# A graph network kernel: the early sorted tile of a step goes behind the first filter layer, in steps that have no same-source sums

## The chip, the cores and the metric

The kernel runs on one core of a Trainium2 chip. The time is the device time of one execution, in microseconds, as the median of three runs; lower is better. Engines are named as in the profile: PE is TensorE, DVE VectorE, ACT ScalarE, POOL GpSimd, SP SyncE.

## The reference

A continuous-filter convolution over a graph of 6250 nodes and 200000 edges, inside a residual block:

```python
h = jnp.maximum(_layernorm(x, axis=-1), 0.0)
x = atomic_embedding @ W_in                                  # atomic_embedding = h
W_ij = shifted_softplus(f_ij @ W_f1 + b_f1) @ W_f2 + b_f2    # 20 -> 128 -> 128 for each edge
W_ij = W_ij * f_ij_cutoff
x_ij = x[idx_j] * W_ij                                       # idx_j = dst, which is sorted
out = jax.ops.segment_sum(x_ij, idx_i, num_segments=N_ATOMS) # idx_i = src, which is not
return shifted_softplus(out @ W_o1 + b_o1) @ W_o2 + b_o2     # and + x at the end
```

## The kernel before

Edges are cut into 391 chunks of 512 (four groups of 128). For each chunk the kernel computes a filter in two layers, fetches the rows of `dst` out of a window of 42 nodes, multiplies both into a message, and adds the message to the rows of `src`. There are two ways for the last part:

- **Pool chunks** (283). TensorE multiplies each group's messages by a matrix that marks equal sources (`same_product`, L1327, the "same-source sums"), ScalarE takes the sums out (`take_sums`: L748 the fourth group, L749 the other three), VectorE makes the target rows (L1011, L1015), and GpSimd scatters them with four indirect DMAs that add into four accumulators in HBM (L613). The scatters of a chunk wait for its sums and its targets; each also waits until the one before it on its accumulator has landed. ScalarE's `take_sums` waits until the scatters of four chunks earlier have landed.
- **PE chunks** (108, those with `c % 25` in `ON_PE`, seven of 25). The messages are sorted into 14 bins on TensorE: seven *tiles* for each chunk, four matmuls of 386 columns each (`bin_up`, L1341), all into the one PSUM bank `binned_ps`. ScalarE empties it after each tile (`take_binned`, L758), and the next tile waits for that (`s_binned`). From the sorted tiles, node sums are made by `add_nodes` (L1360) and added by VectorE (L1059).

The program of each engine is written out step by step. Step `k` on TensorE works on several chunks at once; its order before the change:

1. same-source sums of chunk `k - 2`, if that is a pool chunk; the fourth group waits for the hidden layer of `k`
2. the *early* tile of this step (`late` is 0 in `sorts_at[k]`)
3. `filter_bias` of `k` (L1315, 32 rows, one matmul of 512 columns), which waits for the message of `k - 1` (`s_msg`), since both use bank 2
4. `hidden_product` of `k + 1` (L1307, the first filter layer, 20 rows of fp32)
5. the product with the window of `k` (L1396, 126 rows), then the second filter layer (L1320)
6. node sums (L1360), if a job is due in this step
7. the *late* tile of the step

A table worked out ahead (`sorts_at`, `sums_at`) gives the jobs of each step. In general each step behind a PE chunk's messages has one early and one late tile until its seven are done. Steps whose `k - 2` is a PE chunk have no sums: these are the "steps without same-source sums". 107 of them have an early tile, and in all of these the step before ends with a late tile.

ScalarE's order in step `k`: take the sums of `k - 2` (L748, L749), empty the early tile (L758), softplus of the hidden layer of `k + 1` in three passes (L740, L742, L744), scale the window product of `k` by the cutoff (L782, four), empty the late tile (L758). VectorE's: one-hot of `k + 1` (L1049), node sums added (L1059), targets of `k - 2` (L1011, L1015), positions (L1074), the matrix of equal sources (L1004), positions of tiles (L1041), parts of the payload (L1089, L1094), the last pass of the hidden layer of `k + 1` (L1020), the message of `k` (L1112, or L1109 for a PE chunk).

Behind the last step SyncE waits for the last node sums (`s_dense`) and for all scatters, and reloads the accumulators (L521); then comes the output network.

Of the kernel before, what the change touches and what calls it, by code (L numbers as in the profile page):

```python
# [24 lines left out]
def gnn_kernel(nc, x, src, src_cols, dst, dst_cols, attr_cols, cutoff_cols, W_in, W_f1, b_f1, W_f2, b_f2, W_o1, b_o1, W_o2, b_o2, out):  # L25
# [30 lines left out]
    with ctx:  # L56
# [254 lines left out]
        def on_pe(c):  # L311
            return c in pe_index

        def exists(c):
            return 0 <= c < NCH

        def pool_chunk(c):
            return exists(c) and not on_pe(c)
# [4 lines left out]
        def pool_until(c):  # L323
            return max(0, min(c + 1, NCH)) - pe_until(c)
# [4 lines left out]
        def wait(eng, semaphore, value):  # L329

            if value > 0:
                eng.wait_ge(semaphore, value)

        def after(eng, semaphore, c):

            wait(eng, semaphore, c + 1)
# [15 lines left out]
        def tile_of(kk_slot, i):  # L352

            return (2 * kk_slot + i) % JT

        def place_of(kk_slot, j):

            return (j - 2 * kk_slot) % JT
# [18 lines left out]
        for kk in range(NPE + SLOTS - 1):  # L377
# [7 lines left out]
            for i in tiles_summed(kk):  # L385
                for ages in (OLD, NEW):
                    for d in ages:
                        if holds(kk, d):
                            step, late = sorted_in[kk - d, place_of((kk - d) % SLOTS, tile_of(kk % SLOTS, i))]
# [815 lines left out]
        def _(pe):  # L1205
# [97 lines left out]
            def hidden_product(slot):  # L1303

                for r in range(2):
                    rows = slice(64 * r, 64 * r + RBF)
                    ins = MM(hidden_ps[:, r, :], w_f1[rows, :], attrT[rows, slot, :], start=True, stop=True)  # L1307
                ins.then_inc(s_hp, 1)
# [4 lines left out]
            def filter_bias():  # L1313

                MM(ps[2], ones_bf[BIAS_ROWS, :], bf2_parts[BIAS_ROWS, :, :].rearrange("p t f -> p (t f)"), start=True, stop=False, skip_group_check=True)  # L1315
# [8 lines left out]
            def same_product(odd, tiles):  # L1324

                for t in tiles:
                    ins = MM(sums_ps[t], same[:, odd, t * P:(t + 1) * P], message[:, odd, t, :], start=True, stop=True)  # L1327
                return ins
# [4 lines left out]
            def bin_up(kk, h, i):  # L1333

                j = tile_of(h, i)
                if i == 0:
                    wait(pe, s_pay, kk + 1)
                    wait(pe, s_place[h % 2], T * (kk - h % 2 + 2))
                wait(pe, s_binned, kk * JT + i)
                for t in range(T):  # L1340
                    ins = MM(binned_ps[:, 0:PC], place[:, h % 2, t, j * P:(j + 1) * P], payload_high[:, h % 2, t, :],  # L1341
                             start=(t == 0), stop=(t == T - 1))
                ins.then_inc(s_binps, 1)
# [19 lines left out]
                    ins.then_inc(s_dense, 1)  # L1363

            def hybrid_products():
                def step(k):
                    n = k - 2
                    if pool_chunk(n):
                        wait(pe, s_same, pool_until(n))
                        after(pe, s_msg, n)  # L1370
                        wait(pe, s_s, pool_until(n) - 1)
                        same_product(n % 2, range(T - 1))
                        if exists(n + 2):
                            after(pe, s_h, n + 2)
                        same_product(n % 2, (T - 1,)).then_inc(s_sp, 1)
                    jobs = sorts_at.get(k, ())
                    for kk, h, i, late in jobs:
                        if not late:
                            bin_up(kk, h, i)
                    n = k  # L1380
                    if exists(n):
                        after(pe, s_msg, n - 1)
                        filter_bias()
                    n = k + 1
                    if exists(n) and n > 0:
                        after_slot(pe, s_attr, n, 2)
                        after(pe, s_h, n - 1)
                        wait(pe, s_last_sum, pool_until(n - 3))
                        hidden_product(n % 4)
                    n = k  # L1390
                    if exists(n):
                        after(pe, s_oh, n)
                        after_slot(pe, s_xwin, n)
                        after(pe, s_xg, n - 1)
                        for t in range(T):
                            ins = MM(ps[3][:, t * F:(t + 1) * F], onehot[0:KW, n % 2, t * P:(t + 1) * P],  # L1396
                                     xwin[0:KW, n % 4, :], start=True, stop=True)
                        ins.then_inc(s_xgp, 1)
                        after(pe, s_h, n)
                        filter_product(n % 2)  # L1400
                    for job in sums_at.get(k, ()):
                        add_nodes(*job)
                    for kk, h, i, late in jobs:
                        if late:
                            bin_up(kk, h, i)
                hybrid_steps(step)
# [29 lines left out]
            for q in range(NQ + 2):  # L1436
                if q < NQ:
                    n, h = len(quad(q)), q % 2
# [6 lines left out]
                if 1 <= q < NQ + 1:  # L1445
                    k, h = q - 1, (q - 1) % 2
# [5 lines left out]
                if q >= 2:  # L1452
                    k, h = q - 2, q % 2
# [61 lines left out]
```

## Time and profile before

| | |
|---|---|
| median of three runs | 2326.39 us (2325.42 to 2327.26) |
| profiled execution | 2328.92 us, its span 2327.0 us |
| TensorE busy | 2167.9 us (93%), 16966 matmuls |
| VectorE, ScalarE, GpSimd busy | 1832.7 (79%), 1786.3 (77%), 1851.5 us (80%) |
| granted TensorE clock, mean | 0.979 |

Busy is the time in which an engine has an instruction in execution. The profiled execution is one of its own and stands 2.5 us above the median; its span runs from the first to the last instruction. The granted clock is the share of full speed; between 161 and 2240 us it is 1.00.

### The profile page before, as it was taken

Reading aid. Unit: us, or ns where it says so; the run is one execution under the profiler, and the core shown is the slowest. Engines: PE = TensorE matmul, PEld = TensorE weight load, DVE = VectorE, ACT = ScalarE, POOL = GpSimd, SP = SyncE. Lnnn points to the kernel's source line nnn. Section 1 sums busy time; section 2 is a strip of 40 time slices with the busy share of each in tenths; the row PEclk is TensorE's granted clock in tenths of the full one; section 3 lists DMA queues with packets and bytes.
Section 4 is the critical chain, followed back from the end, with each engine's and each line's share of the span. In section 5 each row is a group of like instructions: output and inputs, shape, how many; then the busy total and the mean of one; then the engine's idle time right before and its main releaser. Section 6 shows DMA issues by size and latency. Waiting matters only on the chain.

```text
span 2327.0 us, 56603 instructions
## 1 busy us (share of the span) xinstructions
PE 2167.9 (93%) x16966; PEld 1364.0 (59%) x16966; DVE 1832.7 (79%) x3906; ACT 1786.3 (77%) x4171; POOL 1851.5 (80%) x1182
## 2 busy tenths in 40 slices
PE   7599999999999999999999999999999999999966
PEld 5456666656666666665665666566666665666533
DVE  7577888778888888888788777878888878887856
ACT  5588888888888788887887888888878878788824
POOL 1488888888888888888888888888888888888863
PEclk9699999999999999999999999999999999999978
DMA  9566566556555656665665565556555666666656
GB/s 334 160 94 92 91 92 89 90 92 91 89 92 90 91 92 90 90 91 91 91 91 90 90 92 93 87 93 93 88 93 92 91 88 91 91 92 90 87 124 236
DMA packets 350175, 239.85 MB, mean 103 GB/s; under 512 B 89295, under 2 KB 337551, under 8 KB 349539
## 3 DMA queue, kind: packets, MB, share of 16 engines
q0 software_dynamic: 164000, 77.47, 34.9%
q1 hardware_dynamic: 184651, 158.26, 25.3%
q8 instruction: 140, 2.29, 0.4%
q14 instruction: 172, 1.41, 0.2%
q10 hardware_dynamic: 1212, 0.42, 0.1%
HBM read 139.86 MB, written 96.12 MB: 101 GB/s over the span
## 4 chain that ended last, share of the span: by engine, by line
DMA 37%; PE 28%; POOL 16%; issue 14%; ACT 2%; SPq 2%; DVE 1%; POOLq 0%; ACTq 0%; DVEq 0%
DMA acc<-region,target 35%; POOL acc L613 15%; PE ps L1341 8%; PE ps L1360 6%; PE ps L1320 5%; PE ps L1327 3%; PE ps L1307 2%; PE ps L1396 2%; PE ps L1315 2%; SPq L459 1%; ACT region L758 1%; DMA w_f<-in_L_gnn_W_f_dram 1%; DMA dst_rows<-region 1%; DMA region<-acc 0%; DMA xw_parts<-region 0%
## 5 line engine op out<-in xcount | busy, mean ns | idle before, releaser
L613 POOL DMA_INDIRECT acc<-region,target x1132 | 1802.8, 1593 | 361.6 <-issue 256.0
L1341 PE MATMUL ps<-region 128*128 128x386 bf16 x3024 | 650.8, 336 | 67.1 <-ACT region L758 65.7
L758 ACT ACTIVATE region<-ps 128x386 bf16<-128x386 f32 x756 | 372.3, 492 | 211.5 <-PE ps L1341 202.9
L1360 PE MATMUL ps<-region 64*128 64x448 bf16 x4536 | 497.9, 352 | 9.4 <-DVE region L1059 9.4
L1341 PEld LDWEIGHTS ps<-region 128*128 128x128 bf16 x3024 | 253.6, 97 | 368.0 <-issue 138.4
L1020 DVE SCALAR_TENSOR_TENSOR region<-ps,bf_negative,region 128x512 f32<-128x512 f32 x391 | 292.4, 748 | 191.3 <-ACT region L744 189.8
L782 ACT ACTIVATE region<-ps,cut_col 128x128 f32<-128x128 f32 x1564 | 439.0, 362 | 0.7 <-PE ps L1396 0.7
L1320 PE MATMUL ps<-w_f,region 128*128 128x128 f32 x3128 | 438.3, 283 | 0.0
L1320 PEld LDWEIGHTS ps<-w_f,region 128*128 128x128 f32 x3128 | 384.0, 193 | 0.0
L740 ACT ACTIVATE region<-ps,bf 128x512 f32<-128x512 f32 x391 | 268.8, 687 | 74.2 <-PE ps L1307 72.0
L1327 PEld LDWEIGHTS ps<-region 128*128 128x128 f32 x2264 | 295.3, 192 | 26.5 <-DVE region L1020 5.0
L1360 PEld LDWEIGHTS ps<-region 64*128 64x128 bf16 x4536 | 191.2, 94 | 197.1 <-issue 14.6
L1327 PE MATMUL ps<-region 128*128 128x129 f32 x2264 | 303.3, 275 | 2.9 <-DVE region L1020 2.9
L1074 DVE TENSOR_SCALAR region<-counting,region 128x448 bf16<-128x448 f16 x756 | 284.0, 416 | 9.1 <-PE ps L1360 8.5
L1307 PE MATMUL ps<-attrT,w_f 20*128 20x256 f32 x1564 | 276.1, 428 | 2.6 <-DVE region L1020 0.6
L1112 DVE TENSOR_TENSOR region<-ps,region 128x512 f32<-128x512 f32 x283 | 195.5, 691 | 78.6 <-ACT region L782 63.1
L742 ACT ACTIVATE region<-region 128x512 f32<-128x512 f32 x391 | 246.8, 631 | 12.5
L744 ACT ACTIVATE region<-region 128x512 f32<-128x512 f32 x391 | 246.2, 630 | 12.4
L1059 DVE TENSOR_TENSOR region<-region,ps 128x896 f32<-128x896 f32 x188 | 202.5, 1077 | 4.3 <-PE ps L1360 4.3
L1004 DVE TENSOR_TENSOR region<-src_b,src_col 128x512 f32<-128x512 int16 x283 | 194.3, 687 | 0.0
L1041 DVE TENSOR_SCALAR region<-counting,place_col 128x896 bf16<-128x896 f16 x432 | 191.0, 462 | 0.0
L1011 DVE TENSOR_SCALAR moved<-region,weight_limit,spare_row 128x4 f32<-128x4 f32 x283 | 97.8, 345 | 107.8 <-ACT region L749 107.8
(136 smaller groups left out, 1616.7 us busy)
## 6 DMA issues: line engine op xcount, KB each, us to landing
dst_b<-dst_rows SPq DMA_DIRECT2D x391, 128.0 KB
src_b<-src_rows SPq DMA_DIRECT2D x283, 128.0 KB
acc<-region,target POOLq DMA_INDIRECT x1132
attrT<-in_edge_attr_dram SPq DMA_DIRECT2D x782, 20.0 KB
acc<-region SPq DMA_DIRECT2D x20, 640.0 KB, 8.5
xwin<-xw_parts SPq DMA_DIRECT2D x391, 31.5 KB
region<-acc SPq DMA_DIRECT2D x48, 256.0 KB, 5.3
xw_parts<-region SPq DMA_DIRECT2D x12, 384.0 KB, 2.3
```

The source lines that it names most:

```text
L613: nc.gpsimd.indirect_dma_start(out=acc[a], out_offset=bass.IndirectOffsetOnAxis(ap=target[:, slot, t:t + 1], axis=0), in_=summed[:, slot, ...
L740: nc.scalar.activation(a, z, ACT.Abs, bias=bias).then_inc(steps[0], 1)
L742: nc.scalar.activation(a, a, ACT.Exp, scale=-1.0).then_inc(steps[1], 1)
L758: nc.scalar.activation(binned[:, h, j, :], binned_ps[:, 0:PC], ACT.Copy).then_inc(s_binned, 1)
L782: last = nc.scalar.activation(xg[:, n % 2, t * F:(t + 1) * F], ps[3][:, t * F:(t + 1) * F], ACT.Copy, scale=cut_col[:, bass.ds(n, 1), t])
L1020: V.scalar_tensor_tensor(halves(hidden[:, odd, :]), hidden_ps, bf1_negative[:, 0:1], halves(hidden_exp[:, odd, :]), ALU.max, ALU.add).then ...
L1074: V.tensor_scalar(in_node[:, sums_until(kk, i) % 2, slot, :], counting[:, 0:NL], binned[:, slot, j, 3 * F:3 * F + 1], binned[:, slot, j, 3 ...
L1307: ins = MM(hidden_ps[:, r, :], w_f1[rows, :], attrT[rows, slot, :], start=True, stop=True)
L1320: ins = MM(ps[2][:, t * F:(t + 1) * F], hidden[:, odd, t * P:(t + 1) * P], w_f2[:, :], start=False, stop=(t == T - 1), skip_group_check=True)
L1327: ins = MM(sums_ps[t], same[:, odd, t * P:(t + 1) * P], message[:, odd, t, :], start=True, stop=True)
L1341: ins = MM(binned_ps[:, 0:PC], place[:, h % 2, t, j * P:(j + 1) * P], payload_high[:, h % 2, t, :], start=(t == 0), stop=(t == T - 1))
L1360: ins = MM(ps[6 + r][:, 0:NL], binned[rows, slot, j, part * F:(part + 1) * F], in_node[rows, sums_until(kk, i) % 2, slot, :], start=(d == ...
```

## The change

In steps whose chunk `k - 2` is a PE chunk (or does not exist), the early tile is issued behind `filter_bias` and `hidden_product` and ahead of the window product. In all other steps the order stays as it was. `ON_PE` and the job tables are the same, and the orders of VectorE, ScalarE, GpSimd and SyncE do not change; ScalarE still empties the early tile ahead of its softplus.

```diff
--- before.py
+++ after.py
@@ -1363,6 +1363,11 @@
                     ins.then_inc(s_dense, 1)
 
             def hybrid_products():
+                def sort_early(jobs):
+                    for kk, h, i, late in jobs:
+                        if not late:
+                            bin_up(kk, h, i)
+
                 def step(k):
                     n = k - 2
                     if pool_chunk(n):
@@ -1374,9 +1379,8 @@
                             after(pe, s_h, n + 2)
                         same_product(n % 2, (T - 1,)).then_inc(s_sp, 1)
                     jobs = sorts_at.get(k, ())
-                    for kk, h, i, late in jobs:
-                        if not late:
-                            bin_up(kk, h, i)
+                    if pool_chunk(k - 2):
+                        sort_early(jobs)
                     n = k
                     if exists(n):
                         after(pe, s_msg, n - 1)
@@ -1387,6 +1391,8 @@
                         after(pe, s_h, n - 1)
                         wait(pe, s_last_sum, pool_until(n - 3))
                         hidden_product(n % 4)
+                    if not pool_chunk(k - 2):
+                        sort_early(jobs)
                     n = k
                     if exists(n):
                         after(pe, s_oh, n)
```

The program of TensorE, first in a step with node sums. L1341 x8 before is the late tile of the step ahead and the early tile of this one; L1396 and L1402 are the same line before and after. Before:

```order
L1360 MATMUL ps<-region 128x448 x12
L1341 MATMUL ps<-region 128x386 x8
L1315 MATMUL ps<-bf_parts,ones_bf 128x512
L1307 MATMUL ps<-attrT,w_f 128x256 x2
L1396 MATMUL ps<-xwin,onehot 128x128 x4
L1320 MATMUL ps<-w_f,region 128x128 x4
L1360 MATMUL ps<-region 128x448 x12
L1341 MATMUL ps<-region 128x386 x4
L1327 MATMUL ps<-region 128x129 x4
```

Of the change:

```order
L1360 MATMUL ps<-region 128x448 x12
L1341 MATMUL ps<-region 128x386 x4
L1315 MATMUL ps<-bf_parts,ones_bf 128x512
L1307 MATMUL ps<-attrT,w_f 128x256 x2
L1341 MATMUL ps<-region 128x386 x4
L1402 MATMUL ps<-xwin,onehot 128x128 x4
L1320 MATMUL ps<-w_f,region 128x128 x4
L1360 MATMUL ps<-region 128x448 x12
L1341 MATMUL ps<-region 128x386 x4
L1327 MATMUL ps<-region 128x129 x4
```

The second four of L1341 have moved from ahead of L1315 to behind L1307. The step behind it, which has sums (L1327), reads as before.

Second, a step without sums that has no node sums either (no L1360), before:

```order
L1341 MATMUL ps<-region 128x386 x8
L1315 MATMUL ps<-bf_parts,ones_bf 128x512
L1307 MATMUL ps<-attrT,w_f 128x256 x2
L1396 MATMUL ps<-xwin,onehot 128x128 x4
L1320 MATMUL ps<-w_f,region 128x128 x4
L1341 MATMUL ps<-region 128x386 x4
L1327 MATMUL ps<-region 128x129 x4
L1341 MATMUL ps<-region 128x386 x4
L1315 MATMUL ps<-bf_parts,ones_bf 128x512
```

Of the change:

```order
L1341 MATMUL ps<-region 128x386 x4
L1315 MATMUL ps<-bf_parts,ones_bf 128x512
L1307 MATMUL ps<-attrT,w_f 128x256 x2
L1341 MATMUL ps<-region 128x386 x4
L1402 MATMUL ps<-xwin,onehot 128x128 x4
L1320 MATMUL ps<-w_f,region 128x128 x4
L1341 MATMUL ps<-region 128x386 x4
L1327 MATMUL ps<-region 128x129 x4
L1341 MATMUL ps<-region 128x386 x4
L1315 MATMUL ps<-bf_parts,ones_bf 128x512
```

The same four matmuls moved; the late tile of this step follows the second filter layer L1320 at once, then come the sums L1327 of the next step and its early tile.

## Rows read from the trace of the kernel before

**Rows 1.** The page, part 4: the chain that ended last, by engine.

```profile
DMA 37%; PE 28%; POOL 16%; issue 14%; ACT 2%; SPq 2%; DVE 1%; POOLq 0%; ACTq 0%; DVEq 0%
```

**Rows 2.** Groups of instructions on GpSimd: busy, mean ns | idle before, its releasers.

```profile
L613 POOL DMA_INDIRECT acc<-region,target x1132 | 1802.8, 1593 | 361.6 <-issue 256.0 <-DMA acc<-region,target 83.8 <-DVE target L1015 20.0
```

**Rows 3.** Timeline, GpSimd: its first and its last scatter.

```profile
103.24 1.81 POOL L613 DMA_INDIRECT acc<-region,target  x1 [16.96 <-DVE target L1015]
...
2249.16 1.55 POOL L613 DMA_INDIRECT acc<-region,target  x1 [0.30 <-issue]
```

**Rows 4.** Waits on TensorE: us in total, times, longest.

```profile
PE ps L1341 <- ACT region L758: 65.7, 107, 1.6
...
PE ps L1327 <- DVE region L1020: 2.9, 11, 0.3
```

**Rows 5.** Timeline: one chunk's target and its first scatter.

```profile
2205.16 0.16 DVE L1015 TENSOR_TENSOR target<-moved,src_col 128x4 int32<-128x4 f32 x1
...
2206.39 1.60 POOL L613 DMA_INDIRECT acc<-region,target  x1 [0.30 <-issue]
```

**Rows 6.** Timelines of TensorE and SyncE: last node sums, first accumulator reloads.

```profile
2248.79 1.30 PE L1360 MATMUL ps<-region 64*128 64x448 bf16 x6 [1.27 <-DVE region L1059]
...
2252.60 6.58 SPq L521 DMA_DIRECT2D region<-acc  x12
```

**Rows 7.** Timeline of a step without sums and the one behind it.

```profile
1003.50 0.87 PE L1341 MATMUL ps<-region 128*128 128x386 bf16 x4
...
1004.22 0.69 DVE L1112 TENSOR_TENSOR region<-ps,region 128x512 f32<-128x512 f32 x1 [0.22 <-issue]
...
1004.95 0.86 PE L1341 MATMUL ps<-region 128*128 128x386 bf16 x4 [0.58 <-ACT region L758]
...
1005.75 0.39 PE L1315 MATMUL ps<-bf_parts,ones_bf 32*128 32x512 bf16 x1
...
1006.38 0.40 PE L1396 MATMUL ps<-xwin,onehot 126*128 126x128 bf16 x4
1006.50 0.69 ACT L740 ACTIVATE region<-ps,bf 128x512 f32<-128x512 f32 x1 [0.15 <-PE ps L1307]
...
1006.61 1.11 PE L1320 MATMUL ps<-w_f,region 128*128 128x128 f32 x8
...
1008.41 1.12 ACT L782 ACTIVATE region<-ps,cut_col 128x128 f32<-128x128 f32 x4
...
1008.90 0.86 PE L1341 MATMUL ps<-region 128*128 128x386 bf16 x4
...
1009.60 1.05 PE L1327 MATMUL ps<-region 128*128 128x129 f32 x8
...
1010.49 0.85 PE L1341 MATMUL ps<-region 128*128 128x386 bf16 x4
...
1011.27 0.39 PE L1315 MATMUL ps<-bf_parts,ones_bf 32*128 32x512 bf16 x1
```

**Rows 8.** Timeline of step 4, without sums and without sorted tiles.

```profile
110.84 0.69 DVE L1112 TENSOR_TENSOR region<-ps,region 128x512 f32<-128x512 f32 x1 [0.33 <-ACT region L782]
...
111.59 0.38 PE L1315 MATMUL ps<-bf_parts,ones_bf 32*128 32x512 bf16 x1 [2.64 <-DVE region L1112]
...
111.69 0.70 PE L1307 MATMUL ps<-attrT,w_f 20*128 20x256 f32 x4
...
112.32 0.40 PE L1396 MATMUL ps<-xwin,onehot 126*128 126x128 bf16 x4
```

**Rows 9.** Timeline: a message that is later against the early tile.

```profile
319.71 0.68 DVE L1112 TENSOR_TENSOR region<-ps,region 128x512 f32<-128x512 f32 x1
...
320.23 0.86 PE L1341 MATMUL ps<-region 128*128 128x386 bf16 x4 [0.59 <-ACT region L758]
```

**Rows 10.** Timeline: early tile of the step behind one without node sums.

```profile
522.10 0.51 ACT L758 ACTIVATE region<-ps 128x386 bf16<-128x386 f32 x1
...
522.66 0.86 PE L1341 MATMUL ps<-region 128*128 128x386 bf16 x4
```

## The prediction

> **What bounds the kernel now.** I read the chain of waits first, then the waits of TensorE, then the scatters on GpSimd, and last the timeline of a few steps. The chain that ended last [rows 1] is the surprise of the page: TensorE is the busiest engine, yet only 28% of the chain lies on it. The rest is scatters: DMA, POOL, and the time in which a scatter is issued. The reader is to see why in [rows 2, 3]. GpSimd runs 1132 scatters, the first from 103.2 us, the last from 2249.2. Of its 361.6 us of idle time 256.0 + 83.8 are the 0.30 that stands ahead of each scatter whatever it waits for (339.8 / 1131), and 20.0 a wait for a target, 17.0 of them ahead of the first. So from its first scatter to its last GpSimd is never without work; the mean from start to start is (2249.2 - 103.2) / 1131 = 1.90 us.
>
> TensorE [rows 4] has one wait of weight in the loop: 65.7 us in 107 places ahead of a sorted tile (L1341) for ScalarE's L758. That is the spot of the change. Outside it TensorE waits for nearly nothing, so whatever the change adds on TensorE delays every later step.
>
> The two engines are thus close to a tie, and two slacks decide what a delay of TensorE does to the end. The first: how long a chunk's target has been ready when its first scatter starts. I compared all 283; the smallest near the end is chunk 277 of them [rows 5], target ready at 2205.32, scatter at 2206.39: **1.1 us** of slack. The second is at the end [rows 6]: TensorE's last node sum ends at 2250.1, and the first reload of an accumulator is issued at 2252.6, after the last scatter has landed: **2.5 us**. A TensorE delay D therefore costs D - 1.1 through the scatters (D - 2.5 through the node sums), and a TensorE that got faster would gain nothing, since GpSimd has no gap to close.
>
> **What the change does, one step.** It moves four matmuls from ahead of the filter bias to behind the first filter layer in 107 steps. No instruction is added or removed, and the queues of the other engines are as they were. Rows of one step are [rows 7]. Before: late tile at 1003.50, its last matmul out by 1004.37; early tile at 1004.95 (0.58 idle, until L758 has emptied the one PSUM bank of both); bias at 1005.75, window product L1396 at 1006.38, so 0.80 for the early tile and 0.63 for bias and first layer.
>
> - *The gap does not close, it changes its owner.* The bias must wait for the message of the chunk before (DVE L1112). That one ends at 1004.22 + 0.69 = 1004.91. Where a bias was held by a message in the trace it started 0.06 behind its end (110.84 + 0.69 = 111.53, bias at 111.59) [rows 8]. So the bias starts at 1004.97 where the early tile started at 1004.95. In 91 of the 107 steps I find this difference between 0.02 and 0.04: **+0.03**.
> - *The run from bias to the next product gets longer.* In the one step without sums that already had its bias held by the message [rows 8], first layer starts 0.10 behind the bias and the window product 0.73 behind it (111.59 to 112.32), against 0.63 in [rows 7], where both wait conditions had been met while the tile ran. I take the same for bias to early tile: **+0.10**.
> - *The early tile itself gets shorter.* A sorted tile followed by the bias takes 0.80 (1004.95 to 1005.75) or 0.78 behind sums; followed by another product on 128 rows it takes 0.70 (1008.90 to 1009.60). After the change the window product on 126 rows follows, and the step from L1396 to L1320 (1006.38 to 1006.61, four of 0.06) shows no such loss between 126 and 128 rows. The loss at the bias (128 rows to 32) now falls into the wait: **-0.09**. Behind the first layer I expect the loss that L1396 has there now, so nothing new.
>
> The Trainium skill has a rule for it, "TensorEngine Tiling (Array Packing)", Key Properties: a change of tiling mode drains TensorE. The trace agrees, 0.80 against 0.70 us. Read so, the number of such changes in a step stays four, but one moves into a wait; without it the step would cost 0.09 more and the sum below about 10 us more.
>
> Net +0.04 per step (to the nanosecond records, 0.035): 107 x 0.035 = **3.7 us**.
>
> - *Steps with a late message.* In 16 steps the message ends later against the tile: [rows 9] has one, 319.71 + 0.68 + 0.06 = 320.45 against 320.23, +0.22. All 16 together: **+4.3 us**, 1.8 of them in the first four steps.
> - *ScalarE.* It still takes the early tile out before it starts L740 of the next chunk. The early tile now ends at 1004.97 + 0.73 + 0.86 = 1006.56, so L758 runs to 1007.1 and L740 starts at 1007.0 (back to back they overlap by 0.1) instead of 1006.50: **+0.5**, and L782 ends at 1010.04 instead of 1009.53. Who needs it? The late tile, done at 1009.76, is emptied from 1009.93 to 1010.42; the next early tile starts at 1010.49 + 0.04 and needs that 0.05 before: it just holds. The next bias needs the message by 1011.3, which would end near 1010.8: holds. In 80 steps of this kind it costs nothing, with under 0.1 us to spare.
> - *Short steps.* Where a step has no node sums the late tile comes sooner, and the next early tile is already held by ScalarE: [rows 10], L758 from 522.10 to 522.61, tile at 522.66. There the 0.5 of ScalarE goes straight through, as it does for VectorE's L1020, which holds L1327 in 11 places [rows 4]. Some 8 or 9 steps x 0.47: **+4 us**.
>
> Sum: D = 3.7 + 4.3 + 4 = 12 us on TensorE, some of the start-up part probably absorbed, so 11.5. At the end 11.5 - 1.1 = **+10.4 us**. The profiled execution took 2328.9 with a span of 2327.0; the median of the runs is 2326.4. 2326.4 + 10.4 = 2336.8, so 2337.
>
> **Rivals.**
> 1. *The 0.10 is not paid* (TensorE's sequencer gets the first layer ready while the bias waits). The Trainium skill, "TensorE: Matmul & The Clock Gate", Step-by-step, speaks for it: weight loads are pulled ahead of running matmuls. No row here shows it past an unmet wait. D falls by 10.7 to 1, which the 1.1 us of slack swallows: 2326 to 2327, no change. For it: one row only carries the price, at the loop's start. 0.14.
> 2. *ScalarE's lateness spreads.* If L740 does not overlap L758, it is 0.13 later, the 80 ordinary steps lose 0.08 each, +6 us: 2343. Or the -0.09 does not come, +10: 2347. Together 0.17.
> 3. *Faster.* The gap of 0.58 really is filled, D = -60 or so. It needs the message 0.5 us sooner, and that is held by ScalarE's L782 (see the releaser in [rows 8]), which the change leaves where it is or delays. And even then GpSimd, busy from 103.2 on, ends where it does: 0 us, no change. Faster at the clock could come only through shorter scatters: their mean of 1.59 us [rows 2] is 0.04 above the 1.55 of an undisturbed one [rows 3], so at most 0.04 x 1132 = 45 us lie there; a tenth of it, 5 us, would have to come back and D stay under 1. 0.03.
> 4. *It does nothing.* TensorE's cost is real but the scatters were the bound all along by more than I think (the low slack of 1.1 us is one chunk; the next lowest are 2 to 2.5). Then +9: inside the forecast.
>
> **How the numbers follow.** No change can be told below 0.2%, 4.7 us, that is D under 5.8. Forecast mechanism 0.66; rival 1 0.14, rival 2 0.17, rival 3 0.03. Same: rival 1 and a small part of the forecast where the short and late steps come out at nothing, 0.18. Slower 0.79, faster 0.03. The range runs from rival 1 (2326) to most of rival 2 (2346).
>
> **What the profile after would show.** The wait of L1341 for L758 falls from 65.7 to a few us, and L1315 waits for L1112 some 70 us in 107 places. In such a step: bias to L1307 0.10, bias to early tile 0.73, early tile to window product 0.70, L740 0.5 later. GpSimd gets real waits, for L1015 or L749, of about 10 us beside those of before, all in the second half, where the slack of [rows 5] is used up. If GpSimd shows no new wait and the time is longer all the same, my end term is wrong; if L1307 stands on the bias with no 0.10, rival 1 holds; if L1341 waits for L758 in more than 20 ordinary steps, rival 2.

## The result and the profile after

| | before | change |
|---|---|---|
| median of three runs | 2326.39 us (2325.42 to 2327.26) | 2342.86 us (2342.25 to 2344.55) |
| profiled execution, its span | 2328.92, 2327.0 us | 2342.86, 2341.0 us |
| TensorE busy; GpSimd busy | 2167.9; 1851.5 us | 2166.2; 1853.8 us |

The ratio is 1.0068, with a 95% interval from 1.0055 to 1.0081: 16.5 us slower by the medians, 14.0 us by the two profiled spans (before's profiled execution stood 2.5 us above its median, this one is the median). The interval in microseconds is 12.8 to 18.8, and the forecast of +10.4 lies below it. What follows explains the 14.0.

The page of the change, part 4 (the chain that ended last, by engine), against [rows 1]:

```profile
PE 66%; ACT 14%; issue 6%; DMA 5%; DVE 5%; POOL 3%; SPq 2%; ACTq 0%; DVEq 0%; POOLq 0%
```

Part 5, the sorted tiles, L1341 (busy, mean ns | idle ahead of it):

```profile
L1341 PE MATMUL ps<-region 128*128 128x386 bf16 x3024 | 651.2, 336 | 1.4
```

Waits of TensorE (us in total, times, longest), against [rows 4]:

```profile
PE ps L1315 <- DVE region L1112: 81.7, 124, 2.6
...
PE ps L1327 <- DVE region L1020: 6.7, 11, 0.7
```

Groups on GpSimd, against [rows 2]:

```profile
L613 POOL DMA_INDIRECT acc<-region,target x1132 | 1805.2, 1595 | 374.0 <-issue 263.6 <-DMA acc<-region,target 72.5 <-DVE target L1015 37.9
```

The wait for ScalarE is gone, 1.4 us of idle time is all that L1341 has left, and the message's wait has taken its place at the bias (3.9 us in 4 places before, 81.7 in 124 after, so some 78 us for the 65.7 removed; L1341's own idle time falls from 67.1 to 1.4). The chain of work that ended last ran through the scatters before; now it runs through TensorE. GpSimd's rows say what that means: its idle time grew by 12.4 us (361.6 to 374.0), nearly all of it real waits for a chunk that isn't ready, and its scatters by 2.4 us.

The timeline of one step without sums and the one behind it, against [rows 7]:

```profile
1011.54 0.87 PE L1341 MATMUL ps<-region 128*128 128x386 bf16 x4
...
1012.27 0.69 DVE L1112 TENSOR_TENSOR region<-ps,region 128x512 f32<-128x512 f32 x1
...
1013.02 0.39 PE L1315 MATMUL ps<-bf_parts,ones_bf 32*128 32x512 bf16 x1 [0.61 <-DVE region L1112]
...
1013.12 0.70 PE L1307 MATMUL ps<-attrT,w_f 20*128 20x256 f32 x4
...
1013.75 0.86 PE L1341 MATMUL ps<-region 128*128 128x386 bf16 x4
...
1014.45 0.39 PE L1402 MATMUL ps<-xwin,onehot 126*128 126x128 bf16 x4
...
1014.65 0.49 ACT L758 ACTIVATE region<-ps 128x386 bf16<-128x386 f32 x1 [1.72 <-PE ps L1341]
...
1015.04 0.68 ACT L740 ACTIVATE region<-ps,bf 128x512 f32<-128x512 f32 x1
...
1017.95 0.51 ACT L758 ACTIVATE region<-ps 128x386 bf16<-128x386 f32 x1
...
1018.55 0.85 PE L1341 MATMUL ps<-region 128*128 128x386 bf16 x4
```

The message ends at 1012.96, and the bias starts 0.06 behind it. The first layer starts 0.10 and the early tile 0.73 behind the bias, the window product 0.70 behind the tile. From the late tile to the window product it is 2.91 us, against 2.88 in [rows 7]. ScalarE starts L740 2.02 behind the place where TensorE went on (the bias), against 1.55 in [rows 7] (the tile), 0.47 later. At the end of the rows L758 is done at 1018.46 and the next early tile starts at 1018.55, 7.01 behind the first row against 6.99 in [rows 7]: ScalarE's 0.47 does not reach it.

Taking the start of the window product in every one of the 391 steps, change minus before, gives TensorE's delay D: 3.3 us at step 20, 4.5 at 50, 5.8 at 100, 9.1 at 200, 12.2 at 300, **14.7 at the last**. By steps: the 107 with the move hold +9.8 (77 of them 0.03 to 0.04, median 0.038, the others up to 0.70), the steps right behind them +4.7 (8 at +0.47, one at +1.54, one at +0.18, some 90 at -0.01), the other 177 only 0.2.

One of the eight, timeline of the change, against [rows 10]:

```profile
527.53 0.49 PE L1327 MATMUL ps<-region 128*128 128x129 f32 x2 [0.74 <-DVE region L1020]
527.59 0.51 ACT L758 ACTIVATE region<-ps 128x386 bf16<-128x386 f32 x1
...
528.16 0.86 PE L1341 MATMUL ps<-region 128*128 128x386 bf16 x4
```

The fourth group's sums wait 0.74 for VectorE's L1020, and the tile behind them is again released by L758. Before, the same wait for L1020 was 0.26.

A late message, timeline of the change:

```profile
971.27 0.73 DVE L1004 TENSOR_TENSOR region<-src_b,src_col 128x512 f32<-128x512 int16 x1
971.28 1.55 POOL L613 DMA_INDIRECT acc<-region,target  x1 [0.30 <-issue]
...
971.93 0.60 DVE L1041 TENSOR_SCALAR region<-counting,place_col 128x896 bf16<-128x896 f16 x1
...
973.78 0.68 DVE L1112 TENSOR_TENSOR region<-ps,region 128x512 f32<-128x512 f32 x1
...
974.51 0.39 PE L1315 MATMUL ps<-bf_parts,ones_bf 32*128 32x512 bf16 x1 [0.76 <-DVE region L1112]
```

Here the bias waits 0.76, not 0.61. VectorE lost it: L1004 took 0.73 and L1041 0.60, where they mostly take 0.68 and 0.44. A scatter runs beside both; but so it does beside most of the L1041 that take 0.44 (311 of the 432 lie wholly inside a scatter, with a mean of 0.47), so being beside one is not enough. In 21 of the 28 late steps of this trace L1041 is 0.15 and L1004 0.05 longer, as here; in the other steps with the move they are 0.02 and 0.00 longer on average.

GpSimd and VectorE near the end, timeline of the change, against [rows 5]:

```profile
2219.07 1.55 POOL L613 DMA_INDIRECT acc<-region,target  x1 [0.30 <-issue]
...
2220.35 0.16 DVE L1015 TENSOR_TENSOR target<-moved,src_col 128x4 int32<-128x4 f32 x1
...
2221.32 1.84 POOL L613 DMA_INDIRECT acc<-region,target  x1 [0.71 <-issue]
```

GpSimd is free at 2220.62, the target ready at 2220.51, and yet the scatter starts at 2221.32. The page calls this "issue"; it is a chunk's start on a GpSimd that had run dry, 0.81 behind the target. Of the 20 chunks that start so in the change, 19 have a distance of 0.80 from target to scatter, one 1.53; no chunk has less than 0.80.

The end, TensorE's last node sum and SyncE's first reload, against [rows 6]:

```profile
2262.54 1.30 PE L1360 MATMUL ps<-region 64*128 64x448 bf16 x6 [1.27 <-DVE region L1059]
...
2267.53 6.44 SPq L521 DMA_DIRECT2D region<-acc  x12
```

The last scatter ends at 2265.8 instead of 2250.7 (+15.1: 2.4 of longer scatters and 12.7 of waiting, nearly all of it in 31 places), the reload follows 14.9 later than before, and what comes behind it took 0.9 less.

### The profile page after: what moved, and what is told of

Its sections match the earlier page's. It is cut to its first block, busy times and chain, and to the rows that moved or that the text cites. A ratio compares the mean times of both kernels' runs of the same rounds, so it can differ in the third digit from the quotient of the medians.

```text
span 2341.0 us, 56603 instructions
## 1 busy us (share of the span) xinstructions
PE 2166.2 (93%) x16966; PEld 1384.6 (59%) x16966; DVE 1835.1 (78%) x3906; ACT 1765.7 (75%) x4171; POOL 1853.8 (79%) x1182
## 4 chain that ended last, share of the span: by engine, by line
PE 66%; ACT 14%; issue 6%; DMA 5%; DVE 5%; POOL 3%; SPq 2%; ACTq 0%; DVEq 0%; POOLq 0%
PE ps L1341 19%; PE ps L1360 13%; PE ps L1320 10%; PE ps L1327 9%; ACT region L782 6%; PE ps L1307 6%; PE ps L1315 5%; ACT region L740 4%; DVE region L1112 4%; ACT region L742 3%; PE ps L1402 3%; DMA acc<-region,target 3%; POOL acc L613 2%; SPq L459 1%; DMA w_f<-in_L_gnn_W_f_dram 1%
## 5 line engine op out<-in xcount | busy, mean ns | idle before, releaser
L613 POOL DMA_INDIRECT acc<-region,target x1132 | 1805.2, 1595 | 374.0 <-issue 263.6
L1341 PE MATMUL ps<-region 128*128 128x386 bf16 x3024 | 651.2, 336 | 1.4
L758 ACT ACTIVATE region<-ps 128x386 bf16<-128x386 f32 x756 | 374.1, 495 | 272.9 <-PE ps L1341 265.8
L1360 PE MATMUL ps<-region 64*128 64x448 bf16 x4536 | 497.8, 352 | 9.0 <-DVE region L1059 9.0
L1020 DVE SCALAR_TENSOR_TENSOR region<-ps,bf_negative,region 128x512 f32<-128x512 f32 x391 | 292.4, 748 | 227.7 <-ACT region L744 221.9
L1320 PE MATMUL ps<-w_f,region 128*128 128x128 f32 x3128 | 439.4, 284 | 0.0
L1341 PEld LDWEIGHTS ps<-region 128*128 128x128 bf16 x3024 | 249.4, 97 | 294.2 <-issue 174.4
L1320 PEld LDWEIGHTS ps<-w_f,region 128*128 128x128 f32 x3128 | 385.0, 194 | 0.0
L1327 PEld LDWEIGHTS ps<-region 128*128 128x128 f32 x2264 | 295.2, 192 | 30.3 <-DVE region L1020 8.8
L740 ACT ACTIVATE region<-ps,bf 128x512 f32<-128x512 f32 x391 | 268.3, 686 | 57.9 <-PE ps L1307 55.8
L1327 PE MATMUL ps<-region 128*128 128x129 f32 x2264 | 303.0, 275 | 6.7 <-DVE region L1020 6.7
L1360 PEld LDWEIGHTS ps<-region 64*128 64x128 bf16 x4536 | 191.2, 94 | 196.4 <-issue 13.9
L1074 DVE TENSOR_SCALAR region<-counting,region 128x448 bf16<-128x448 f16 x756 | 289.4, 423 | 8.7 <-PE ps L1360 8.1
L1307 PE MATMUL ps<-attrT,w_f 20*128 20x256 f32 x1564 | 276.0, 426 | 0.7 <-DVE region L1020 0.6
L744 ACT ACTIVATE region<-region 128x512 f32<-128x512 f32 x391 | 246.3, 630 | 12.4
L1315 PE MATMUL ps<-bf_parts,ones_bf 32*128 32x512 bf16 x391 | 151.0, 386 | 92.0 <-DVE region L1112 81.7
L1041 DVE TENSOR_SCALAR region<-counting,place_col 128x896 bf16<-128x896 f16 x432 | 193.9, 469 | 0.0
L1004 DVE TENSOR_TENSOR region<-src_b,src_col 128x512 f32<-128x512 int16 x283 | 193.9, 685 | 0.0
```

What stands on the lines that cost most here:

```text
L613: nc.gpsimd.indirect_dma_start(out=acc[a], out_offset=bass.IndirectOffsetOnAxis(ap=target[:, slot, t:t + 1], axis=0), in_=summed[:, slot, ...
L740: nc.scalar.activation(a, z, ACT.Abs, bias=bias).then_inc(steps[0], 1)
L758: nc.scalar.activation(binned[:, h, j, :], binned_ps[:, 0:PC], ACT.Copy).then_inc(s_binned, 1)
L1020: V.scalar_tensor_tensor(halves(hidden[:, odd, :]), hidden_ps, bf1_negative[:, 0:1], halves(hidden_exp[:, odd, :]), ALU.max, ALU.add).then ...
L1074: V.tensor_scalar(in_node[:, sums_until(kk, i) % 2, slot, :], counting[:, 0:NL], binned[:, slot, j, 3 * F:3 * F + 1], binned[:, slot, j, 3 ...
L1320: ins = MM(ps[2][:, t * F:(t + 1) * F], hidden[:, odd, t * P:(t + 1) * P], w_f2[:, :], start=False, stop=(t == T - 1), skip_group_check=True)
```

## The experiments

Diffs are parts of the edits, against the change unless it is said otherwise; "..." stands for lines left out. "D" is TensorE's delay against before, made as above, in the one profiled execution of each kernel. Each kernel is compared with runs of before on its own chip: their median was 2327.33 us for e1 to e4, 2329.31 for e5 to e8 and 2328.26 for e9 to e11, so that only the ratios compare across these three groups. The step of [rows 7], from the start of its late tile to its window product, measures 2.88 us before, and in the others (of e9 the median of the 107):

| kernel | the step, us | median, us | ratio to before (95%) |
|---|---|---|---|
| change | 2.91 | 2342.86 | 1.0068 (1.0055 to 1.0081) |
| softplus first on ScalarE (e1) | 2.91 | 2335.74 | 1.0038 (1.0023 to 1.0052) |
| waits ahead of the bias (e2) | 2.91 | 2342.42 | 1.0060 (1.0046 to 1.0074) |
| first layer, tile, bias (e3) | 2.56 | 2325.02 | 0.9989 (0.9980 to 0.9999) |
| bias, tile, first layer (e4) | 3.23 | 2370.50 | 1.0190 (1.0174 to 1.0206) |
| message's wait alone (e5) | 2.81 | 2341.00 | 1.0042 (1.0029 to 1.0056) |
| e1 and e5 together (e9) | 2.81 | 2335.70 | 1.0032 (1.0020 to 1.0043) |

**Softplus first (e1).** ScalarE empties the early tile behind the first pass of the softplus.

```diff
-                    for kk, h, i, late in jobs:
-                        if not late:
-                            take_binned(kk, h, i)
...
-                        softplus(hidden_ps, bf1[:, 0:1], halves(hidden_exp[:, n % 2, :]), (s_size, s_exp, s_log), n + 1)
+                        softplus(hidden_ps, bf1[:, 0:1], halves(hidden_exp[:, n % 2, :]), (s_size, s_exp, s_log), n + 1,
+                                 take_early if behind else lambda: None)
```

> The change as it is, but ScalarE empties the early tile behind the first pass of its softplus (L740) instead of ahead of it, in steps without sums. My theory: the early tile no longer delays ScalarE's chain, so the 0.47 us of the 8 steps behind steps without node sums and the 1.54 us of step 9 go, about 5 us: 2338 us. The 0.04 us of the ordinary steps and the late messages stay. Rival (all of the cost is TensorE's own order, ScalarE has no share): 2343 us, no difference.

Its timeline in the short step (L1314 is the first layer here, L1322 the bias, L759 the emptying):

```profile
520.79 0.38 PE L1322 MATMUL ps<-bf_parts,ones_bf 32*128 32x512 bf16 x1 [0.67 <-DVE region L1119]
...
521.63 0.69 ACT L740 ACTIVATE region<-ps,bf 128x512 f32<-128x512 f32 x1 [0.97 <-PE ps L1314]
...
522.42 0.49 ACT L759 ACTIVATE region<-ps 128x386 bf16<-128x386 f32 x1
...
522.81 0.62 ACT L743 ACTIVATE region<-region 128x512 f32<-128x512 f32 x1
```

L740 starts 0.84 behind the bias, not 2.02. The eight short steps went from +0.47 to -0.26 each, 5.8 us back; D ends at 7.5, 7.2 less (1.5 of it stands there already at the first step, from the start-up of this execution). The 107 steps with the move stayed (+10.2, median 0.040). So the short steps are ScalarE's lateness, and ordinary steps owe it nothing. By the ratios e1 took 7 us less than the change, and the two intervals do not touch. Step 9's +1.54 stayed as well, though I had put it down to ScalarE; more on it below.

**Waits ahead of the bias (e2).** The first layer's three waits (attributes, `s_h`, `s_last_sum`), long met, are issued ahead of the bias's wait for the message.

```diff
+                    n = k + 1
+                    if not pool_chunk(k - 2) and exists(n) and n > 0:
+                        after_slot(pe, s_attr, n, 2)
+                        after(pe, s_h, n - 1)
+                        wait(pe, s_last_sum, pool_until(n - 3))
                     n = k
                     if exists(n):
                         after(pe, s_msg, n - 1)
...
-                        after_slot(pe, s_attr, n, 2)
-                        after(pe, s_h, n - 1)
-                        wait(pe, s_last_sum, pool_until(n - 3))
+                        if pool_chunk(k - 2):
+                            after_slot(pe, s_attr, n, 2)
+                            after(pe, s_h, n - 1)
+                            wait(pe, s_last_sum, pool_until(n - 3))
                         hidden_product(n % 4)
```

> The change as it is, but in steps without sums TensorE waits for what the first layer needs (attributes, hidden layer, last sums) ahead of the bias, together with the message; all three were there long before. My theory: the 0.10 us between L1315 and L1307 is the sequencer handling the first layer's wait conditions only after the bias has been let go; it falls to near 0, 107 x 0.10 = 10 us: 2333 us. Rival: it is a fixed cost of starting again after a stall, and stays: 2343 us.

```profile
1014.34 0.37 PE L1315 MATMUL ps<-bf_parts,ones_bf 32*128 32x512 bf16 x1 [0.70 <-DVE region L1112]
1014.34 0.70 PE L1307 MATMUL ps<-attrT,w_f 20*128 20x256 f32 x4
1014.97 0.86 PE L1341 MATMUL ps<-region 128*128 128x386 bf16 x4
1015.68 0.39 PE L1408 MATMUL ps<-xwin,onehot 126*128 126x128 bf16 x4
```

(Its timeline of TensorE; L1408 is the window product.) The first layer now stands on the bias, and the tile 0.63 behind it: the 0.10 is gone from there. But the bias waits 0.70 instead of 0.61: it starts 0.15 behind the message instead of 0.06. The time moved by less than the intervals can tell. The price had changed its place, which neither theory had foreseen.

**The message's wait alone (e5).** My reading of e2 was that the waits gathered ahead of the bias still stood together with the message's, so that the last of them was an instruction of its own. An increment of an unused semaphore behind the first layer's waits gathers them, and the message's wait sits on the bias again. The diff is against e2.

```diff
                         wait(pe, s_last_sum, pool_until(n - 3))
+                        pe.sem_inc(s_pe_go, 1)
                     n = k
                     if exists(n):
                         after(pe, s_msg, n - 1)
```

> As the run with the waits ahead, but the bias is left with the message as its only wait: in steps without sums a semaphore increment by the sequencer stands between the first layer's wait conditions and the message's. In the run before it the 0.10 us had only moved: L1307 stood on the bias, but the bias started 0.15 us behind the message instead of 0.06. My theory (the price is one more wait instruction handled after the release): bias 0.06 behind the message and L1307 on the bias, 0.10 x 107 = 10 us less than the change: 2333 us. Rival (a fixed restart price of 0.16 us in whatever place): 2342 us.

Its timeline of TensorE (L1316 bias, L1308 first layer, L1342 tile, L1410 window product):

```profile
1090.78 0.38 PE L1316 MATMUL ps<-bf_parts,ones_bf 32*128 32x512 bf16 x1 [0.61 <-DVE region L1113]
1090.78 0.70 PE L1308 MATMUL ps<-attrT,w_f 20*128 20x256 f32 x4
1091.41 0.86 PE L1342 MATMUL ps<-region 128*128 128x386 bf16 x4
1092.11 0.39 PE L1410 MATMUL ps<-xwin,onehot 126*128 126x128 bf16 x4
```

Now both are there: 0.61 of wait and 0.63 from bias to tile. TensorE's weight loads show the same, first in the change and then here:

```profile
1013.01 0.09 PEld L1315 LDWEIGHTS ps<-bf_parts,ones_bf 32*128 32x128 bf16 x1 [1.02 <-DVE region L1112]
1013.09 0.33 PEld L1307 LDWEIGHTS ps<-attrT,w_f 20*128 20x128 f32 x4
```

```profile
1090.77 0.09 PEld L1316 LDWEIGHTS ps<-bf_parts,ones_bf 32*128 32x128 bf16 x1 [1.02 <-DVE region L1113]
1090.78 0.30 PEld L1308 LDWEIGHTS ps<-attrT,w_f 20*128 20x128 f32 x4
```

The first layer's load starts 0.08 behind the bias's in the change and 0.01 behind it here. The 107 steps sum to -4.1 us (median -0.062, against +0.038): the 0.10 was one wait instruction worked through behind a release. Yet by the ratios the kernel won only 6 us, with intervals that touch: the other 177 steps, untouched in the change, lost 8.5, and from the start of the first scatter to the end of the last GpSimd took 2162.2 us, the change 2162.3, before 2147.5. Its groups:

```profile
L614 POOL DMA_INDIRECT acc<-region,target x1132 | 1817.1, 1605 | 362.0 <-issue 254.6 <-DMA acc<-region,target 78.9 <-DVE target L1016 24.2
```

The added waits are gone (362.0, as before's 361.6), but the scatters take 1605 ns for 1593, 14.3 us in all. From the 40th pool chunk on GpSimd lags 5 to 12 us behind its targets in nine chunks of ten, so it is the scatters that set the end again, not TensorE; what was won there had nowhere to go. **Both mends (e9)** together:

> The change with both mends: ScalarE empties the early tile behind the first pass of its softplus, and the bias is left with the message as its only wait. On TensorE alone the 107 steps should cost 0.06 us less than in the kernel before and the 8 short ones 0.26 less, some 8 us in all. My theory: GpSimd, without a gap, then sets the end: 2327 us if its scatters take 1.593 us on average as before, up to 2341 if they take 1.605 as in the run with the message alone. Rival (TensorE sets the time): 2319 us.

It measured 2335.70: the 107 steps -3.2, the short ones -0.26 each, 10.6 given back in other steps, scatters 1602 ns. It lands where e1 does, and above before. What makes the scatters longer in some kernels and not in others I cannot say. That e5 and e9 ran on another chip than e1 to e4 is not enough: e4's scatters took 1606 ns, and before was only 2 us slower on e5's chip than on e4's.

**First layer, tile, bias (e3), and bias, tile, first layer (e4).** What the message need not hold up goes ahead of it, or one more product goes behind it:

```diff
...
+                    else:
+                        first_layer()
                         sort_early(jobs)
+                        bias_product()
```

and in e4:

```diff
...
+                    else:
+                        bias_product()
                         sort_early(jobs)
+                        first_layer()
```

> In steps without sums the order on TensorE is first layer, early tile, bias, window product. The first layer waits for nothing new and fills the 0.58 us in which the early tile waits for ScalarE; the bias then no longer runs beside it. By the rows of before: first layer 0.8 us behind the start of the late tile, early tile at 1.45, bias 0.8 later, window product 0.35 later, 2.6 us against 2.88 before: TensorE gains some 0.28 us a step, 30 us in all. My theory (GpSimd has no gap to close before either): the end stays where it was in the kernel before, 2325 to 2328 us. Rival (TensorE sets the time): 2297 us.

Its timeline of TensorE in such a step:

```profile
1017.74 0.86 PE L1341 MATMUL ps<-region 128*128 128x386 bf16 x4
1018.53 0.70 PE L1307 MATMUL ps<-attrT,w_f 20*128 20x256 f32 x4
1019.18 0.86 PE L1341 MATMUL ps<-region 128*128 128x386 bf16 x4
1019.98 0.38 PE L1315 MATMUL ps<-bf_parts,ones_bf 32*128 32x512 bf16 x1
1020.30 0.40 PE L1408 MATMUL ps<-xwin,onehot 126*128 126x128 bf16 x4
```

No wait is left. The 107 steps are 25.5 us shorter (median -0.316), and the kernel is only 0.1% faster: 18 us were given back in other steps (3.2 of them in steps 9 and 23, where the granted clock was at its lower level, as in step 9 of the change below). GpSimd's group reads 1803.5 us busy and 360.9 idle, as before's 1802.8 and 361.6, and its last scatter starts 2146.8 us behind its first (100.38 to 2247.19), against 2145.9 in [rows 3]. GpSimd has no gap to close, and it passes its pace back: ScalarE may take a chunk's sums only when the scatters of four chunks earlier have landed, and TensorE waits for ScalarE in turn (1.40 for L748 at 899.69 us). ScalarE's list of waits in e3 (36.1 us, longest 1.0, in before):

```profile
ACT region L748 <- DMA acc<-region,target: 60.8, 89, 3.1
```

> In steps without sums: bias, early tile, first layer, window product; only the bias goes ahead of the tile. My theory: the bias (32 rows) and the first layer (20 rows) run at the same time when they stand side by side; apart, the bias costs 0.3 us of its own and there are two more changes between 32 and 128 rows. By the rows: 0.61 + 0.35 + 0.80 + 0.63 = 2.39 us from the end of the late tile to the window product against 2.02 before, +0.37 x 107 = 40 us: 2366 us. Rival (only the wait for the message counts, the order of the rest is free): 2343 us as the change.

```profile
1022.06 0.87 PE L1341 MATMUL ps<-region 128*128 128x386 bf16 x4
1023.54 0.39 PE L1315 MATMUL ps<-bf_parts,ones_bf 32*128 32x512 bf16 x1 [0.61 <-DVE region L1112]
1023.86 0.86 PE L1341 MATMUL ps<-region 128*128 128x386 bf16 x4
1024.65 0.70 PE L1307 MATMUL ps<-attrT,w_f 20*128 20x256 f32 x4
1025.29 0.40 PE L1408 MATMUL ps<-xwin,onehot 126*128 126x128 bf16 x4
```

The wait is the same 0.61, but bias and first layer no longer run side by side, and a tile stands between: 0.32 + 0.79 + 0.64 = 1.75 from bias to window product, against 0.73 + 0.70 = 1.43 in the change. The 107 steps cost 41.1 us, D ends at 41.7, and the time is within 4.5 us of what the sum of such rows had said.

**A quarter of the scatters left out (e6 to e8, e10, e11).** To take GpSimd out of the tie, the fourth group of each pool chunk isn't scattered and nothing waits for its accumulator, so the output lacks these sums; everything else is as it was. e6 is before in this form, e7 and e11 the change, e8 the order of e3, e10 that of e5.

```diff
-                        for t in range(T):
+                        for t in range(T - 1):
```

> The kernel before, with the scatter of the fourth group of each pool chunk left out (849 scatters instead of 1132, nothing waits for the fourth accumulator); the sums of these groups are missing from the output. GpSimd needs 849 x 1.9 = 1613 us, so TensorE sets the time. My theory: TensorE's path ended only 2.5 us ahead of the scatters' in the kernel before, so 2323 to 2326 us. Rival (the scatters were the bound by much more): under 2310 us.

> The change, with the fourth group's scatters left out as in the run beside it. My theory: TensorE's delay of 14.7 us comes out whole, 2338 to 2341 us; a little less than that if fewer scatters disturb VectorE's passes and so fewer messages are late. Rival (the loss came from the scatters): no difference to the light kernel before.

> First layer, early tile, bias, window product in steps without sums, with the fourth group's scatters left out. With all scatters this order gained TensorE 25.5 us in its steps and the end 2 us only. My theory: with GpSimd out of the way the gain comes through, 0.3 x 107 = 32 us less than the light kernel before: 2293 us. Rival (the gain was lost on ScalarE or VectorE and not to the scatters): 2320 us or more.

Before in this form took 2325.64 us, 3.7 under before on the same chip (ratio 0.9979, 0.9969 to 0.9988): without the load on GpSimd, before's TensorE order would end at about the same place. It was a tie within 4 us. The change took 2335.25, 9.6 more than light before; D, here against light before, is 10.6. (The two profiled spans are only 5.9 apart: e7's profiled execution is 2.1 below its median, e6's 1.6 above. Behind the last step the granted clock was at its lower level for 17 us at a stretch in e7 and for 31 us in e6.) Its ordinary steps have the same median (0.036), and the short steps the same 0.47. But the 107 steps sum to 6.0, not 9.8: most late messages are gone. And e3's order took 2294.7, **31 us less** than light before. Its groups on GpSimd:

```profile
L613 POOL DMA_INDIRECT acc<-region,target x849 | 1381.0, 1627 | 743.2 <-DVE target L1015 478.8 <-issue 190.0 <-DMA acc<-region,target 74.4
```

Now GpSimd waits 479 us for targets, and TensorE's gain arrives at the end: the 107 steps are 29.5 us shorter, and the others give nothing back, where they gave back 18 with all scatters. That is the test of the pace said above.

> The run with the message alone, with the fourth group's scatters left out as in the light runs, to see its order without GpSimd as the bound. My theory: 107 x 0.10 = 10.5 us less than the light change, that is the light kernel before or up to 1 us faster: 2325 us. Rival (that order costs TensorE something that the steps I looked at don't show): 2335 us as the light change.

> The light change once more, beside the light message-alone run on the same chip. 2335 us by the first time; every theory expects the same. It is here for the comparison.

The wait alone, with light scatters, took 2324.36 us (ratio 0.9982, 0.9973 to 0.9991), the light change on the same chip 2335.47 (1.0032, 1.0022 to 1.0043): 11.1 us apart, where 107 x 0.10 = 10.7. In this form what TensorE gains or loses arrives at the end.

## Why the prediction was right, and where its sizes were off

- **The gap changes its owner, +0.03; the bias's run, +0.10; the tile's, -0.09.** Right in each row: 0.06 behind the message, 0.10 to L1307, 0.73 to the tile, 0.70 for the tile. Forecast 3.7 us, measured 107 x 0.038 = 4.1. Rival 1 is refuted as to the change itself, since L1307 does not stand on the bias, but its mechanism exists all the same: e2 and e5 show the first layer on the bias as soon as no wait instruction stands between. The Trainium skill, "TensorE: Matmul & The Clock Gate", Step-by-step, has weight loads pulled ahead of matmuls in flight. The trace agrees in e5, where the first layer's load starts 0.01 behind the bias's. In the change it starts 0.08 behind, with an instruction between them that only waits and whose condition was met.
- **Steps with a late message, +4.3: undersized.** They hold the rest of the 9.8, 5.8 us. 28 messages came late against 16 in the trace of before, which I had counted as if they stayed the same ones; only 11 did. With a quarter of the scatters gone the same sum is 2.2, 7 messages come late, and none of them behind a longer L1041 and L1004, as 21 of the 28 do. So behind the start-up most of the lateness arises in these two passes, and with the full number of scatters only. Why a scatter lengthens some passes and not others stays open.
- **ScalarE 0.5 later, free in ordinary steps.** Right. L740 came 0.47 later, no early tile waits for L758 in the list of waits, and e1, which takes the lateness away, leaves the 107 steps at 0.040. Rival 2 is refuted.
- **Short steps, +4.** Right: eight times 0.47, 3.8 us, and e1 turned them into -0.26. The size of one step behind was not foreseen, +1.54 in step 9. The windows of the change, then of before, then of e11 (length; busy time of PE, PEld, DVE, ACT, POOL; granted clock; DMA share; GB/s):

```profile
133.00:136.50 3.50, 3.50 (x20) 2.16 (x18) 0.90 (x2) 3.36 (x8) 2.89 (x3) 0.51 0.65 121
```

```profile
133.00:136.50 3.50, 3.22 (x27) 2.16 (x27) 1.79 (x4) 3.23 (x10) 2.89 (x3) 1.00 0.65 125
```

```profile
131.00:136.00 5.00, 4.46 (x36) 3.05 (x33) 2.38 (x5) 4.36 (x11) 2.22 (x2) 1.00 0.57 111
```

  The granted clock was 0.51 there, that is the lower of TensorE's two levels, 1.2 GHz, where before had the full 2.4. TensorE had stood idle for 1.96 us ahead of the bias at 131.38, for the message, and was then at work without a gap; the second layer took 2.00 us there instead of 1.11. Two profiled executions of one kernel tell the fall's share: e7 has it in this place and step 9 at +1.53, e11 has the full clock there, behind the same 1.96 of idle time, and +0.39. So some 1.1 us are the clock, and 0.39 is one more short step of ScalarE's: e9, with the full clock and ScalarE's mend, has -0.01. What makes the clock fall in one execution and not in the other isn't shown.
- **End = D - 1.1: the rule held, its slack was wrong.** I took the 1.07 from target to scatter [rows 5] as slack. The change shows 0.80 as what a scatter needs behind its target on an idle GpSimd, so only 0.27 was slack. The signature "all in the second half" fell: GpSimd's added waits begin at 155 us, and 5.5 us of them lie in the first half. That there are such waits, and about 10 us of them, was right.
- **The sum.** Forecast +10.4, measured +14.0 by the spans: D 14.7 for 11.5 (+1.5 late messages, +1.1 clock, +0.4 ordinary steps, +0.2 short ones with step 9, -0.5 in other places, and the 0.5 that I had hoped would be absorbed), slack 0.3 for 1.1, +0.5 of longer scatters beyond that, 0.9 less behind the reload. The mechanism was right, and its terms were too small by 3.6 us in all by the spans. The medians give 16.5, with 14 inside the interval and the forecast's 10.4 outside it; before's profiled execution stood 2.5 above its median, and this is as far as it can be told.
- **Rival 3, "a faster TensorE gains nothing".** Held, more sharply than I had put it: e3 takes 25.5 us out of TensorE's 107 steps and gets 0.1% (ratio 0.9989, at most 0.9999); with a quarter of the scatters left out the same order gets 31 us. Its other half, that the gap of 0.58 can't be filled, holds for the change's place of the tile only. e3 fills it, with the first layer, which the message does not hold up.

No version with all its scatters beats before by more than about a tenth of a per cent. For that the 1132 scatters, 1.90 us each from start to start, would have to become fewer or shorter.

## What to carry to other kernels

A wait that is moved off an instruction uncovers the next one: read the end of the second producer before filling a gap, and put ahead of the wait the work that doesn't depend on it (e3, -0.32 a step), not behind it (e4, +0.35). Where two engines are within a few microseconds of a tie, as here, a delay on either is paid nearly in full (the change on TensorE, e5 on GpSimd) and a gain on TensorE alone is nearly lost (e3); leaving out part of the other's work shows it (e8). The time from a producer's end to its consumer's start isn't slack until the least such time has been taken off, and that is read from a place where the consumer was idle.

## What the runs showed of the hardware that I had not expected

- On a GpSimd that had run dry, a scatter started 0.80 us behind the end of the VectorE operation that made its targets, in 19 places of the change (1.53 in one), and nowhere sooner; the profile books part of it as "issue".
- One wait instruction on TensorE whose condition had long been met cost 0.10 us when it was worked through behind another's release. Issued ahead, it moved the price to the bias (e2); gathered ahead by an increment between, it cost nothing (e5).
- A bias of 32 rows and a first layer of 20 rows ran side by side: the tile came 0.63 behind the start of both. With the tile between them they took 0.32 and 0.64 in turn (e4).
- VectorE's L1041 took over 0.47 us in 63 places of before and 94 of the change (often 0.60), else 0.44; L1004 over 0.71 in 37 and 26, else 0.68. With a quarter of the scatters left out it was 4 and 1 in before, 43 and 1 in the change. Most passes beside a scatter were not longer.
- TensorE's granted clock fell to the lower level at about 131 us in one execution of a kernel (e7) and not in another (e11), behind the same idle time of 1.96 us; the fall cost 1.1 us.
- The mean scatter took 1593 to 1598 ns in before, the change, e1, e2 and e3, and 1602 to 1606 in e4, e5 and e9, with the same data. At 1132 scatters the two groups are 5 to 15 us apart; the cause stays open.
